# The second layer's feed-forward: one straight program for four token blocks instead of a loop with a barrier per block

## Chip, cores and metric

The kernel runs on one NeuronCore of a Trainium2 chip. The metric is the device time of one execution in microseconds (us), and less is better. TensorE is the matrix engine (PE in the profile, with PEld for its weight loads), VectorE is DVE, ScalarE is ACT, GpSimd is POOL and SyncE is SP.

## What is computed

The reference is a stack of four layers with sixteen sublayers on 2048 tokens of 128 features. After every sublayer its result is added to the running sum `x`. The change touches one sublayer, which occurs twice (after each of the second layer's two attentions):

```python
h = silu(x @ w1.T * w1_s) * (x @ w2.T * w2_s)      # 128 -> 512, "gates" and "ups"
h = gelu(h @ h1.T * h1_s)                          # 512 -> 512
h = gelu(h @ h2.T * h2_s)                          # 512 -> 512
x = x + (h @ w3.T) * w3_s                          # 512 -> 128
```

The `x` on the right of the first line is the layer-normalised running sum. The weights hold -1, 0 and 1, and everything is in float32.

## The kernel before

The running sum `X` and its normalised copy `XN` stay on chip, transposed: 128 features on the partitions and 2048 tokens along the free axis. A block is 512 tokens, so there are four blocks (`NBLK`). PSUM is one tensor `PS` with 8 banks of 128x512 float32. A float32 matmul of 128x128 weights with 128x512 tokens shows in the trace as two MATMUL records, with a weight load ahead of each.

**Stages.** The whole kernel is a sequence of stages. A stage (`stage`, line 70) gives each engine a program of its own and ends in a barrier of all engines that also clears the stage's semaphores (line 77, or line 79 for a stage without semaphores). Within a stage the engines are ordered by semaphores alone. Each engine works its own program off in order, and TensorE does not pass a matmul that waits.

**The sublayer.** `l1_ffn` (line 1133) first calls `layernorm` (line 110), a stage of its own whose last instruction is the product on VectorE at line 166. Then a hardware loop (`Fori`, line 1142) runs four times, and its body is one stage, so a barrier stands between two blocks. One block holds 44 float32 matmuls:

- TensorE: gates into banks 0 to 3 and ups into banks 4 to 7, alternating (lines 1148 and 1149, 8 matmuls); the first hidden product into banks 0 to 3 (line 1154, 16); the second hidden product into banks 4 to 7 (line 1159, 16); the last product into bank 0 (line 1163, 4).
- ScalarE: silu of the gates (line 1170), gelu after the first hidden product (line 1173) and after the second (line 1177). Silu and gelu use different function tables, so each block has two table loads.
- VectorE: the gated product of silu and ups into `HA` (line 1183), and at the end the addition to `X` (line 1186).

`l1_ffn` is called twice from `program`. After the first call comes the second attention of the layer, after the second call the next layer's feed-forward weights are loaded and the third layer begins. The SP queue and GpSimd have nothing to do in `l1_ffn` but the barriers. The weights were loaded long before.

Of the kernel before, what the change touches and what calls it, by code (L numbers as in the profile page):

```python
# [15 lines left out]
F32 = mybir.dt.float32  # L16
BF16 = mybir.dt.bfloat16
U32 = mybir.dt.uint32
ALU = mybir.AluOpType
ACT = mybir.ActivationFunctionType  # L20
AX = mybir.AxisListType

P = 128
# [3 lines left out]
NTOK = BATCH * SEQ  # L27
BLK = 512
NBLK = NTOK // BLK
# [39 lines left out]
@contextmanager  # L69
def stage(nc, *names):  # L70


    with ExitStack() as st:
        sems = [st.enter_context(nc.semaphore(n, num=STAGE_SEMS + i)) for i, n in enumerate(names)]
        yield (Programs(nc), *sems)
        if sems:
            nc.all_engine_barrier(sems_to_clear=range(STAGE_SEMS, STAGE_SEMS + len(sems)))  # L77
        else:
            nc.all_engine_barrier()


def blk(i, n=BLK):
    return slice(i * n, (i + 1) * n)
# [1047 lines left out]


def l1_ffn(k):

    nc, PS, W = k.nc, k.PS, k.W
    C = 4
    layernorm(k, k.X, k.XN)
    with ExitStack() as st:
        G = k.sbuf(st, "l1f_G", [P, C, BLK], F32)
        HA = k.sbuf(st, "l1f_HA", [P, C, BLK], F32)  # L1140
        HB = k.sbuf(st, "l1f_HB", [P, C, BLK], F32)
        with nc.Fori(0, NTOK - BLK + 1, BLK) as tb:
            with stage(nc, "g_ready", "g_done", "a_done", "h1_ready", "h1_done", "h2_ready", "h2_done", "y_ready", "added") as (block, g_ready, g_done, a_done, h1_ready, h1_done, h2_ready, h2_done, y_ready, added):
                @block.tensor
                def _(pe):
                    xn = k.XN[:, bass.ds(tb, BLK)]
                    for c in range(C):
                        nc.tensor.matmul(PS[:, c, :], W["L1_ffn_w1"][:, blk(c, P)], xn, start=True, stop=True)
                        nc.tensor.matmul(PS[:, 4 + c, :], W["L1_ffn_w2"][:, blk(c, P)], xn, start=True, stop=True).then_inc(g_ready, 1)
                    for c in range(C):  # L1150
                        pe.wait_ge(g_done, c + 1)
                        for q in range(C):
                            pe.wait_ge(a_done, q + 1)
                            mm = nc.tensor.matmul(PS[:, c, :], W["L1_ffn_h1"][:, q, blk(c, P)], HA[:, q, :], start=(q == 0), stop=(q == C - 1))  # L1154
                        mm.then_inc(h1_ready, 1)
                    for c in range(C):
                        for q in range(C):
                            pe.wait_ge(h1_done, q + 1)
                            mm = nc.tensor.matmul(PS[:, 4 + c, :], W["L1_ffn_h2"][:, q, blk(c, P)], HB[:, q, :], start=(q == 0), stop=(q == C - 1))  # L1159
                        mm.then_inc(h2_ready, 1)  # L1160
                    for q in range(C):
                        pe.wait_ge(h2_done, q + 1)
                        mm = nc.tensor.matmul(PS[:, 0, :], W["L1_ffn_w3"][:, q, :], G[:, q, :], start=(q == 0), stop=(q == C - 1))  # L1163
                    mm.then_inc(y_ready, 1)

                @block.scalar
                def _(act):
                    for c in range(C):
                        act.wait_ge(g_ready, c + 1)
                        nc.scalar.activation(G[:, c, :], PS[:, c, :], ACT.Silu, scale=W["L1_ffn_w1_s"][:, c:c + 1]).then_inc(g_done, 1)  # L1170
                    for c in range(C):
                        act.wait_ge(h1_ready, c + 1)
                        nc.scalar.activation(HB[:, c, :], PS[:, c, :], ACT.Gelu, scale=W["L1_ffn_h1_s"][:, c:c + 1]).then_inc(h1_done, 1)
                    for c in range(C):
                        act.wait_ge(h2_ready, c + 1)
                        act.wait_ge(a_done, c + 1)
                        nc.scalar.activation(G[:, c, :], PS[:, 4 + c, :], ACT.Gelu, scale=W["L1_ffn_h2_s"][:, c:c + 1]).then_inc(h2_done, 1)

                @block.vector
                def _(dve):  # L1180
                    for c in range(C):
                        dve.wait_ge(g_done, c + 1)
                        nc.vector.scalar_tensor_tensor(out=HA[:, c, :], in0=PS[:, 4 + c, :], scalar=W["L1_ffn_w2_s"][:, c:c + 1], in1=G[:, c, :], op0=ALU.mult, op1=ALU.mult).then_inc(a_done, 1)
                    dve.wait_ge(y_ready, 1)
                    xb = k.X[:, bass.ds(tb, BLK)]
                    nc.vector.scalar_tensor_tensor(out=xb, in0=PS[:, 0, :], scalar=W["L1_ffn_w3_s"], in1=xb, op0=ALU.mult, op1=ALU.add).then_inc(added, 1)  # L1186
                    dve.wait_ge(added, 1)


def l2_ffn(k):  # L1190
# [5 lines left out]
    with ExitStack() as st:  # L1196
        G = k.sbuf(st, "l2f_G", [P, C + 1, BLK], F32)
        H = k.sbuf(st, "l2f_H", [P, C + 1, BLK], F32)
        with nc.Fori(0, NTOK - BLK + 1, BLK) as tb:
            with stage(nc, "up_ready", "g_done", "h_half", "h_done", "y_ready", "added") as (block, up_ready, g_done, h_half, h_done, y_ready, added):  # L1200
# [20 lines left out]
                def _(act):  # L1221
                    for c in range(C + 1):
                        act.wait_ge(up_ready, c + 1)
                        nc.scalar.activation(G[:, c, :], PS[:, 3 * (c % 2), :], ACT.Silu).then_inc(g_done, 1)

# [646 lines left out]
def l3a(k):  # L1872

    nc, PS, W = k.nc, k.PS, k.W
    with ExitStack() as st:
        def sb(n, shape, dt=F32):
            return k.sbuf(st, n, shape, dt)
# [3 lines left out]
        S = sb("l3a_s", [P, P])  # L1881
        TRI, HB, CMASK, RMASK = sb("l3a_tri", [P, P]), sb("l3a_hb", [P, P]), sb("l3a_cmask", [P, 4, P]), sb("l3a_rmask", [P, 4])

        def layer_constants(pool, own):
            own(pool.memset(TRI[:, :], 1.0))
            own(pool.affine_select(out=TRI[:, :], in_=TRI[:, :], compare_op=ALU.is_ge, fill=0.0, base=0, pattern=[[1, P]], channel_multiplier=-1))

            own(pool.memset(HB[:, :], 1.0))
            hb = HB[:, :].rearrange("p (h d) -> p h d", d=8)
            own(pool.affine_select(out=hb, in_=hb, compare_op=ALU.is_ge, fill=0.0, base=0, pattern=[[-8, 16], [0, 8]], channel_multiplier=1))  # L1890
# [3 lines left out]
            for s in range(4):  # L1894
                own(pool.memset(CMASK[:, s, :].rearrange("p (g d) -> p g d", g=4)[:, :, 8 * s:8 * s + 8], 1.0))
            hs = HB[:, :].rearrange("p (g s d) -> p g s d", g=4, s=4)
            own(pool.tensor_tensor(RMASK[:, :], hs[:, 0, :, 0], hs[:, 1, :, 0], ALU.add))
# [2420 lines left out]
def program(nc, ins, out, first=0, last=16):  # L4318
# [3 lines left out]
    k.filled_count, k.fetched_count = 0, [0] * 8  # L4322
    run = {"l0a": l0a, "l0b": l0b, "l1a": l1a, "l1b": l1b, "l2a": l2a, "l2b": l2b, "l3a": l3a, "l3b": l3b,
           "l0_ffn": l0_ffn, "l1_ffn": l1_ffn, "l2_ffn": l2_ffn, "l3_ffn": l3_ffn}
    with ExitStack() as st:
        k.X = k.sbuf(st, "X", [P, NTOK])
# [159 lines left out]
```

## Time and profile before

| | |
|---|---|
| runs | 3692.92 us median of 3 (3684.45 to 3695.07) |
| the profiled execution's own time | 3704.39 us |
| its span in the trace | 3702.6 us |
| mean granted TensorE clock | 0.861 of full |
| TensorE busy | 2894.2 us (78%) |
| VectorE busy | 1883.8 us (51%) |
| ScalarE busy | 1402.6 us (38%) |
| GpSimd busy | 774.7 us (21%) |

The profile is one execution. Its page gives shares of the whole span; for a change in one sublayer the timeline, the table of stretches and the list of waits around that sublayer say more. In the trace the two calls of the loop stand at about 1614 to 1779 us and 2330 to 2492 us. The matmuls overlap, since they are pipelined: the end of a MATMUL record is modelled, and the distance between two starts is the rate.

### The profile page before, as it was taken

To read this page: it belongs to the slowest core of one execution; us is meant where nothing else is said; L and a number is where in the kernel's file an instruction comes from. 1 tells how busy PE (TensorE), PEld (TensorE's weight loads), DVE (VectorE), ACT (ScalarE), POOL (GpSimd) and SP (SyncE) were. 2 spreads that over 40 slices of the span, in tenths; PEclk is the share of its full clock that TensorE was granted. 3 is DMA by queue.
4 is the path that set the end of the run, shared out by engine and by line. 5 is a ranking of instruction groups with operands and counts; after the bars stand their busy time and mean duration, and the time that the engine had idled before them with its cause. 6 is when DMAs were issued, how large, how long until landed. Compare 5 with 4: busy or idle time off the path is not lost. (4 is left out here: it accounts for less than half of the span.)

```text
span 3702.6 us, 55144 instructions
## 1 busy us (share of the span) xinstructions
PE 2894.2 (78%) x21390; PEld 1513.0 (41%) x21458; DVE 1883.8 (51%) x3574; ACT 1402.6 (38%) x2678; POOL 774.7 (21%) x631
## 2 busy tenths in 40 slices
PE   6566777778877599989768888998878568777986
PEld 3454247423367334434322222332333333554545
DVE  4311253388953388710488877103953543626733
ACT  3211423433233256632366776323122112234652
POOL 1000006146526200000544320003610000240003
PEclk9666879878878789989889999997999779887987
DMA  2022001122111412000132200000600001014202
GB/s 105 15 68 65 0 16 42 34 75 68 40 27 42 114 36 41 15 0 0 28 53 31 30 2 1 0 11 26 161 7 0 0 0 46 13 54 79 46 11 68
DMA packets 86471, 136.29 MB, mean 37 GB/s; under 512 B 13319, under 2 KB 52199, under 8 KB 84947
## 3 DMA queue, kind: packets, MB, share of 16 engines
q1 hardware_dynamic: 79187, 118.50, 13.0%
q0 software_dynamic: 7040, 14.43, 1.5%
q8 instruction: 165, 2.70, 0.3%
q14 instruction: 79, 0.65, 0.1%
HBM read 106.81 MB, written 25.85 MB: 36 GB/s over the span
## 5 line engine op out<-in xcount | busy, mean ns | idle before, releaser
L1608 ACT ACTIVATE at_pt<-PS 128x384 f32<-128x384 f32 (+3 forms) x704 | 288.7, 455 | 237.4 <-PE PS L1520 202.1
L1658 DVE TENSOR_REDUCE at_mp<-PS 128x1 f32<-128x384 f32 (+3 forms) x640 | 313.5, 538 | 114.9 <-PE PS L1508 98.8
L1505 PE MATMUL PS<-at_kx,at_qx 72*128 72x384 bf16 (+5 forms) x640 | 219.0, 347 | 66.7 <-DMA at_kx<-L_attn_a_parts 26.7
L1518 PE MATMUL PS<-at_qx,at_kx 105*128 105x512 bf16 (+5 forms) x704 | 214.4, 314 | 7.8 <-ACT at_pt L1608 5.9
L4146 DVE CUSTOM_DVE_ANT_0 PS<-PS,ls_pt 128x1024 f32<-128x1024 f32 x128 | 153.9, 1239 | 18.4 <-ACT ls_pt L3999 15.6
L3999 ACT ACTIVATE ls_pt<-PS,ls_far 128x512 f32<-128x512 f32 x256 | 155.0, 686 | 20.4 <-PE PS L3820 11.7
L2271 DVE TENSOR_TENSOR_SCAN mb_ring<-PS,mb_ring 128x1024 f32<-128x1024 f32 x64 | 146.6, 2291 | 18.9 <-POOL mb_ring L2210 6.7
L2226 PE MATMUL PS<-mb_ring,ident 128*128 128x512 f32 x256 | 147.2, 727 | 6.1 <-DVE mb_ring L2276 6.0
L989 ACT ACTIVATE mx_h<-PS,small_L 128x128 f32<-128x128 f32 x312 | 88.2, 372 | 151.5 <-PE PS L873 60.7
L873 PE MATMUL PS<-mx_g,mx_w 128*128 128x128 f32 x624 | 100.7, 313 | 50.9 <-DVE mx_w L1066 24.9
L2255 ACT ACTIVATE PS<-mb_dt,mb_a 128x1024 f32<-128x1024 f32 x64 | 71.6, 1118 | 174.8 <-DVE mb_ring L2271 169.5
L1531 PE MATMUL PS<-at_pt,at_v 128*9 128x256 f32 (+3 forms) x1408 | 130.7, 451 | 5.5 <-issue 1.4
L1520 PE MATMUL PS<-at_above,identb 128*128 128x128 bf16 x704 | 133.8, 223 | 0.0
L1508 PE MATMUL PS<-at_above,identb 128*128 128x128 bf16 x704 | 131.5, 233 | 0.0
L1505 PEld LDWEIGHTS PS<-at_kx,at_qx 102*128 102x128 bf16 (+1 forms) x640 | 64.7, 101 | 159.7 <-DVE at_mp L1658 85.2
L1186 DVE SCALAR_TENSOR_TENSOR X<-PS,small_L,X 128x512 f32 x8 | 6.0, 751 | 236.2 <-PE PS L1163 236.2
L873 PEld LDWEIGHTS PS<-mx_g,mx_w 128*128 128x128 f32 x624 | 90.9, 224 | 58.3 <-DVE mx_w L1066 49.8
L1154 PE MATMUL PS<-l1f_HA,ffn_place 128*128 128x512 f32 x256 | 111.2, 592 | 0.0
L1159 PE MATMUL PS<-l1f_HB,ffn_place 128*128 128x512 f32 x256 | 111.2, 592 | 0.0
L166 DVE TENSOR_TENSOR XN<-PS,lnA 128x512 f32<-128x512 f32 x56 | 38.7, 692 | 138.6 <-ACT lnA L148 138.6
L2217 PE MATMUL PS<-mb_xd,mb_selc 40*128 40x512 f32 x128 | 71.3, 681 | 41.2 <-DVE mb_ring L2276 31.1
L3827 PE MATMUL PS<-ls_kx,ls_qx 96*128 96x512 bf16 x256 | 79.1, 391 | 29.0 <-DVE ls_mp L4146 24.0
(803 smaller groups left out, 6545.8 us busy)
## 6 DMA issues: line engine op xcount, KB each, us to landing
rw_arena<-rw_v_rows SPq DMA_DIRECT2D x32, 512.0 KB, 4.7
dl_arena<-in_fir_bank SPq DMA_DIRECT2D x32, 256.0 KB, 3.1
lnA<-mb_rows SPq DMA_DIRECT2D x16, 512.0 KB, 3.7
XN<-mb_rows SPq DMA_DIRECT2D x16, 512.0 KB, 3.6
ffn_place<-in_ffn_L SPq DMA_DIRECT2D x4, 1152.0 KB, 17.3
at_qx<-L_attn_a_parts SPq DMA_DIRECT2D x24, 192.0 KB
at_kx<-L_attn_a_parts SPq DMA_DIRECT2D x72, 64.0 KB
at_qx<-L_attn_b_parts SPq DMA_DIRECT2D x24, 192.0 KB
```

What stands on the lines that cost most here:

```text
L873: mm = nc.tensor.matmul(PS[:, n % 4, blk(c, P)], W1[:, n % 3, blk(c, P)], XG[:, n % 2, :], start=True, stop=True)
L1505: mm = nc.tensor.matmul(PS[:, n % 3, 0:e - c], QX[0:RAW, u % 3, g, blk(i, P)], KX[0:RAW, u % 3, g, c:e], start=True, stop=True)
L1508: mm = nc.tensor.matmul(PS[:, n % 3, j * P - c:(j + 1) * P - c], k.identb[:, :], ABOVE[:, 0 if j >= i else 1, :], start=False, stop=True, ...
L1518: mm = nc.tensor.matmul(PS[:, 3 + n % 3, 0:e - c], KX[0:FULL, u % 3, g, blk(j, P)], QX[0:FULL, u % 3, g, c:e], start=True, stop=True)
L1520: mm = nc.tensor.matmul(PS[:, 3 + n % 3, i * P - c:(i + 1) * P - c], k.identb[:, :], ABOVE[:, 1 if i <= j else 0, :], start=False, stop=Tr ...
L1531: mm = nc.tensor.matmul(PS[32 * g:32 * g + 9, 6, c - BLK * h:e - BLK * h], V1[:, NT * (u // 4) + j, HG * (u % 4) + g, :], PT[:, (G2 * u + ...
L1608: nc.scalar.activation(PT[:, y % SLOTS, g, 0:e - c], PS[:, 3 + n % 3, 0:e - c], ACT.Exp, scale=SCALE).then_inc(exp_done, 1)
L1658: nc.vector.tensor_reduce(best, sc, AX.X, ALU.max).then_inc(s_maxed, 1)
L2226: mm = nc.tensor.matmul(PS[:, 2 * h + t, :], k.ident[:, :], HC[:, m % 3, blk(t)], start=(n == 0), stop=(n == NS - 1))
L2271: nc.vector.tensor_tensor_scan(HS, wide(6), BU[:, m % 3, :], 0.0, ALU.mult, ALU.add).then_inc(scanned, 1)
L3999: nc.scalar.activation(PT[x % 4][:, blk(t)], PS[:, 4 + (2 * x + t) % 3, :], ACT.Relu, bias=far[:, 0:1], scale=NEG).then_inc(pen_done, 1)
L4146: nc.vector.tensor_tensor_reduce(wide(bank), wide(bank), PT[x % 4], 1.0, -3e38, ALU.subtract, ALU.max, MP[:, u % 2, i // HALF, g, i % HALF ...
```

## The change

The loop and the barrier after each block go. Each engine gets one program over all four blocks, inside one stage, with semaphore values that count on from block to block. There is one more buffer, `S`, for the silu, which shared `G` before. On TensorE the next block's gates stand ahead of the last product of the block before (`gates`, `third`, `ups`, `first`, `second`), and the ups follow that product. The ups now go to banks 5, 6, 7 and 4, and the last product goes to bank 4 in place of bank 0. The additions to `X` stand on VectorE ahead of the next block's gated products. The diff, with removed lines that are in the listing above left out:

```diff
@@ -1131,60 +1131,107 @@
 def l1_ffn(k):
...
     nc, PS, W = k.nc, k.PS, k.W
     C = 4
     layernorm(k, k.X, k.XN)
     with ExitStack() as st:
-        G = k.sbuf(st, "l1f_G", [P, C, BLK], F32)
-        HA = k.sbuf(st, "l1f_HA", [P, C, BLK], F32)
-        HB = k.sbuf(st, "l1f_HB", [P, C, BLK], F32)
-        with nc.Fori(0, NTOK - BLK + 1, BLK) as tb:
-            with stage(nc, "g_ready", "g_done", "a_done", "h1_ready", "h1_done", "h2_ready", "h2_done", "y_ready", "added") as (block, g_ready, g_done, a_done, h1_ready, h1_done, h2_ready, h2_done, y_ready, added):
...
-                    xn = k.XN[:, bass.ds(tb, BLK)]
+        S, HA, HB, G = (k.sbuf(st, "l1f_" + n, [P, C, BLK], F32) for n in ("S", "HA", "HB", "G"))
+        UP_BANK = (5, 6, 7, 4)
+        with stage(nc, "s_ready", "s_done", "up_ready", "a_done", "h1_ready", "h1_done", "h2_ready", "h2_done", "y_ready", "added") as (block, s_ready, s_done, up_ready, a_done, h1_ready, h1_done, h2_ready, h2_done, y_ready, added):
+            @block.tensor
+            def _(pe):
+                def gates(b):
                     for c in range(C):
...
+                        if b:
+                            pe.wait_ge(h1_done, C * (b - 1) + c + 1)
+                        nc.tensor.matmul(PS[:, c, :], W["L1_ffn_w1"][:, blk(c, P)], k.XN[:, blk(b)], start=True, stop=True).then_inc(s_ready, 1)
+                def ups(b):
                     for c in range(C):
...
+                        if b:
+                            pe.wait_ge(h2_done, C * (b - 1) + C)
+                        if b and c == C - 1:
+                            pe.wait_ge(added, b)
+                        nc.tensor.matmul(PS[:, UP_BANK[c], :], W["L1_ffn_w2"][:, blk(c, P)], k.XN[:, blk(b)], start=True, stop=True).then_inc(up_ready, 1)
+                def first(b):
+                    for c in range(C):
+                        pe.wait_ge(s_done, C * b + c + 1)
                         for q in range(C):
...
+                            pe.wait_ge(a_done, C * b + q + 1)
                             mm = nc.tensor.matmul(PS[:, c, :], W["L1_ffn_h1"][:, q, blk(c, P)], HA[:, q, :], start=(q == 0), stop=(q == C - 1))
                         mm.then_inc(h1_ready, 1)
+                def second(b):
                     for c in range(C):
                         for q in range(C):
...
+                            pe.wait_ge(h1_done, C * b + q + 1)
                             mm = nc.tensor.matmul(PS[:, 4 + c, :], W["L1_ffn_h2"][:, q, blk(c, P)], HB[:, q, :], start=(q == 0), stop=(q == C - 1))
                         mm.then_inc(h2_ready, 1)
+                def third(b):
                     for q in range(C):
...
+                        pe.wait_ge(h2_done, C * b + q + 1)
+                        mm = nc.tensor.matmul(PS[:, 4, :], W["L1_ffn_w3"][:, q, :], G[:, q, :], start=(q == 0), stop=(q == C - 1))
                     mm.then_inc(y_ready, 1)
...
+                for b in range(NBLK):
+                    gates(b)
+                    if b:
+                        third(b - 1)
+                    ups(b)
+                    first(b)
+                    second(b)
+                third(NBLK - 1)
+            @block.scalar
+            def _(act):
+                def silu(b):
                     for c in range(C):
...
+                        act.wait_ge(s_ready, C * b + c + 1)
+                        if b:
+                            act.wait_ge(a_done, C * (b - 1) + c + 1)
+                        nc.scalar.activation(S[:, c, :], PS[:, c, :], ACT.Silu, scale=W["L1_ffn_w1_s"][:, c:c + 1]).then_inc(s_done, 1)
+                def first(b):
                     for c in range(C):
...
+                        act.wait_ge(h1_ready, C * b + c + 1)
+                        if b and c == 0:
+                            act.wait_ge(h2_ready, C * b)
                         nc.scalar.activation(HB[:, c, :], PS[:, c, :], ACT.Gelu, scale=W["L1_ffn_h1_s"][:, c:c + 1]).then_inc(h1_done, 1)
+                def second(b):
                     for c in range(C):
...
+                        act.wait_ge(h2_ready, C * b + c + 1)
+                        if b and c == 0:
+                            act.wait_ge(y_ready, b)
                         nc.scalar.activation(G[:, c, :], PS[:, 4 + c, :], ACT.Gelu, scale=W["L1_ffn_h2_s"][:, c:c + 1]).then_inc(h2_done, 1)
...
+                for b in range(NBLK):
+                    silu(b)
+                    first(b)
+                    second(b)
+            @block.vector
+            def _(dve):
+                def product(b):
                     for c in range(C):
...
-                    xb = k.X[:, bass.ds(tb, BLK)]
...
+                        dve.wait_ge(s_done, C * b + c + 1)
+                        dve.wait_ge(up_ready, C * b + c + 1)
+                        if b and c == 0:
+                            dve.wait_ge(h1_ready, C * b)
+                        nc.vector.scalar_tensor_tensor(out=HA[:, c, :], in0=PS[:, UP_BANK[c], :], scalar=W["L1_ffn_w2_s"][:, c:c + 1], in1=S[:, c, :], op0=ALU.mult, op1=ALU.mult).then_inc(a_done, 1)
+                def add(b):
+                    dve.wait_ge(y_ready, b + 1)
+                    nc.vector.scalar_tensor_tensor(out=k.X[:, blk(b)], in0=PS[:, 4, :], scalar=W["L1_ffn_w3_s"], in1=k.X[:, blk(b)], op0=ALU.mult, op1=ALU.add).then_inc(added, 1)
+                for b in range(NBLK):
+                    if b:
+                        add(b - 1)
+                    product(b)
+                add(NBLK - 1)
+                dve.wait_ge(added, NBLK)
 def l2_ffn(k):
```

## Rows read from the trace of the kernel before

**Rows 1.** The page: the head, and busy us by engine.

```profile
span 3702.6 us, 55144 instructions
...
PE 2894.2 (78%) x21390; PEld 1513.0 (41%) x21458; DVE 1883.8 (51%) x3574; ACT 1402.6 (38%) x2678; POOL 774.7 (21%) x631
```

**Rows 2.** Stretches, one per block; columns: busy us by engine, granted clock, DMA share, GB/s.

```profile
1655.50:1697.30 41.80, 39.73 (x88) 17.21 (x88) 3.75 (x5) 10.82 (x14) 0.00 (x0) 0.96 0.00 0
1697.30:1737.30 40.00, 38.03 (x88) 16.64 (x88) 3.75 (x5) 10.81 (x14) 0.00 (x0) 1.00 0.00 0
...
2450.30:2492.00 41.70, 39.73 (x88) 17.23 (x88) 3.76 (x5) 10.81 (x14) 0.00 (x0) 0.96 0.00 0
```

**Rows 3.** Timeline, first seam of call 1; columns: start, duration, engine, instruction, [idle before].

```profile
1650.96 3.60 PE L1163 MATMUL PS<-l1f_G,ffn_place 128*128 128x512 f32 x8
...
1651.17 0.69 ACT L1177 ACTIVATE l1f_G<-PS,small_L 128x512 f32<-128x512 f32 x1 [2.75 <-PE PS L1159]
...
1654.70 0.75 DVE L1186 SCALAR_TENSOR_TENSOR X<-PS,small_L,X 128x512 f32 x1 [29.53 <-PE PS L1163]
...
1656.61 1.83 PE L1148 MATMUL PS<-XN,ffn_place 128*128 x2 [2.04 <-PEq L77]
...
1665.27 13.90 PE L1154 MATMUL PS<-l1f_HA,ffn_place 128*128 128x512 f32 x32
```

**Rows 4.** Timeline, call 1, block 3: its first matmuls and its first hidden product.

```profile
1698.34 1.12 PE L1148 MATMUL PS<-XN,ffn_place 128*128 x2 [2.01 <-PEq L77]
...
1705.31 13.90 PE L1154 MATMUL PS<-l1f_HA,ffn_place 128*128 128x512 f32 x32
```

**Rows 5.** Line 1148, whole kernel: what ended TensorE's idle time before it.

```profile
  PEq L77: 17.8, 8
```

**Rows 6.** Timeline, block 1 of both calls: layernorm's end, first matmuls, hidden products, table load, last gated product.

```profile
1612.36 0.69 DVE L166 TENSOR_TENSOR XN<-PS,lnA 128x512 f32<-128x512 f32 x1 [0.64 <-ACT lnA L148]
...
1613.80 2.07 PE L1148 MATMUL PS<-XN,ffn_place 128*128 x2 [2.86 <-PEq L77]
...
1623.50 13.90 PE L1154 MATMUL PS<-l1f_HA,ffn_place 128*128 128x512 f32 x32
...
1624.40 1.28 ACT L1173 ACT_TABLE_LOAD   x1
1624.42 0.75 DVE L1183 SCALAR_TENSOR_TENSOR l1f_HA<-PS,small_L,l1f_G 128x512 f32<-128x512 f32 x1 [0.97 <-ACT l1f_G L1170]
...
1637.23 13.90 PE L1159 MATMUL PS<-l1f_HB,ffn_place 128*128 128x512 f32 x32
...
2329.80 2.07 PE L1148 MATMUL PS<-XN,ffn_place 128*128 x2 [2.85 <-PEq L77]
...
2338.20 13.90 PE L1154 MATMUL PS<-l1f_HA,ffn_place 128*128 128x512 f32 x32
```

**Rows 7.** Timeline, the last addition of call 1 and of call 2.

```profile
1778.22 0.75 DVE L1186 SCALAR_TENSOR_TENSOR X<-PS,small_L,X 128x512 f32 x1 [29.52 <-PE PS L1163]
...
2491.22 0.75 DVE L1186 SCALAR_TENSOR_TENSOR X<-PS,small_L,X 128x512 f32 x1 [29.52 <-PE PS L1163]
```

**Rows 8.** Short stretches over the first seam of call 1 (columns as in rows 2).

```profile
1654.40:1656.60 2.20, 0.16 (x1) 0.00 (x0) 0.75 (x1) 0.42 (x1) 0.00 (x0) 1.00 0.00 0
1656.60:1658.60 2.00, 1.99 (x3) 0.96 (x4) 0.00 (x0) 0.86 (x1) 0.00 (x0) 0.57 0.00 0
1658.60:1660.60 2.00, 2.00 (x4) 0.72 (x3) 0.00 (x0) 0.41 (x1) 0.00 (x0) 0.58 0.00 0
```

**Rows 9.** Long dense stretches of other sublayers, and one full of instructions (columns as in rows 2).

```profile
2000.00:2300.00 300.00, 261.73 (x1343) 84.37 (x1366) 246.25 (x332) 222.51 (x389) 85.46 (x32) 1.00 0.13 19
3390.00:3510.00 120.00, 113.86 (x1238) 70.72 (x1245) 81.10 (x204) 74.39 (x191) 0.00 (x0) 1.00 0.27 45
...
100.00:200.00 100.00, 62.62 (x3086) 53.79 (x3087) 26.88 (x43) 19.05 (x31) 0.00 (x0) 0.72 0.05 15
```

**Rows 10.** DMA queues, 100 to 200 us: kind, packets, MB, share of 16 engines.

```profile
q8 instruction: 24, 0.39, 1.6%
```

More of the change, by code:

```diff
@@ L1138, in l1_ffn @@
     with ExitStack() as st:
-        G = k.sbuf(st, "l1f_G", [P, C, BLK], F32)
-        HA = k.sbuf(st, "l1f_HA", [P, C, BLK], F32)
-        HB = k.sbuf(st, "l1f_HB", [P, C, BLK], F32)
-        with nc.Fori(0, NTOK - BLK + 1, BLK) as tb:
-            with stage(nc, "g_ready", "g_done", "a_done", "h1_ready", "h1_done", "h2_ready", "h2_done", "y_ready", "added") as (block, g_ready, g_done, a_done, h1_ready, h1_done, h2_ready, h2_done, y_ready, added):
-                @block.tensor
-                def _(pe):
-                    xn = k.XN[:, bass.ds(tb, BLK)]
+        S, HA, HB, G = (k.sbuf(st, "l1f_" + n, [P, C, BLK], F32) for n in ("S", "HA", "HB", "G"))
@@ L1147, in _ @@
+        UP_BANK = (5, 6, 7, 4)
[3 more added lines that the diff above has]
+                def gates(b):
                     for c in range(C):
-                        nc.tensor.matmul(PS[:, c, :], W["L1_ffn_w1"][:, blk(c, P)], xn, start=True, stop=True)
@@ L1149, in _ @@
-                        nc.tensor.matmul(PS[:, 4 + c, :], W["L1_ffn_w2"][:, blk(c, P)], xn, start=True, stop=True).then_inc(g_ready, 1)
+                        if b:
+                            pe.wait_ge(h1_done, C * (b - 1) + c + 1)
+                        nc.tensor.matmul(PS[:, c, :], W["L1_ffn_w1"][:, blk(c, P)], k.XN[:, blk(b)], start=True, stop=True).then_inc(s_ready, 1)
+                def ups(b):
                     for c in range(C):
-                        pe.wait_ge(g_done, c + 1)
+                        if b:
[3 more added lines that the diff above has]
+                        nc.tensor.matmul(PS[:, UP_BANK[c], :], W["L1_ffn_w2"][:, blk(c, P)], k.XN[:, blk(b)], start=True, stop=True).then_inc(up_ready, 1)
@@ L1152, in _ @@
+                def first(b):
+                    for c in range(C):
+                        pe.wait_ge(s_done, C * b + c + 1)
                         for q in range(C):
-                            pe.wait_ge(a_done, q + 1)
+                            pe.wait_ge(a_done, C * b + q + 1)
                             mm = nc.tensor.matmul(PS[:, c, :], W["L1_ffn_h1"][:, q, blk(c, P)], HA[:, q, :], start=(q == 0), stop=(q == C - 1))
                         mm.then_inc(h1_ready, 1)
+                def second(b):
@@ L1156, in _ @@
                     for c in range(C):
                         for q in range(C):
-                            pe.wait_ge(h1_done, q + 1)
+                            pe.wait_ge(h1_done, C * b + q + 1)
                             mm = nc.tensor.matmul(PS[:, 4 + c, :], W["L1_ffn_h2"][:, q, blk(c, P)], HB[:, q, :], start=(q == 0), stop=(q == C - 1))
                         mm.then_inc(h2_ready, 1)
+                def third(b):
                     for q in range(C):
-                        pe.wait_ge(h2_done, q + 1)
@@ L1163, in _ @@
-                        mm = nc.tensor.matmul(PS[:, 0, :], W["L1_ffn_w3"][:, q, :], G[:, q, :], start=(q == 0), stop=(q == C - 1))
+                        pe.wait_ge(h2_done, C * b + q + 1)
+                        mm = nc.tensor.matmul(PS[:, 4, :], W["L1_ffn_w3"][:, q, :], G[:, q, :], start=(q == 0), stop=(q == C - 1))
                     mm.then_inc(y_ready, 1)
-                @block.scalar
-                def _(act):
-                    for c in range(C):
-                        act.wait_ge(g_ready, c + 1)
-                        nc.scalar.activation(G[:, c, :], PS[:, c, :], ACT.Silu, scale=W["L1_ffn_w1_s"][:, c:c + 1]).then_inc(g_done, 1)
+                for b in range(NBLK):
[5 more added lines that the diff above has]
+                    second(b)
@@ L1171, in _ @@
+                third(NBLK - 1)
+            @block.scalar
+            def _(act):
+                def silu(b):
+                    for c in range(C):
+                        act.wait_ge(s_ready, C * b + c + 1)
[3 more added lines that the diff above has]
+                def first(b):
                     for c in range(C):
-                        act.wait_ge(h1_ready, c + 1)
+                        act.wait_ge(h1_ready, C * b + c + 1)
+                        if b and c == 0:
+                            act.wait_ge(h2_ready, C * b)
@@ L1173, in _ @@
                         nc.scalar.activation(HB[:, c, :], PS[:, c, :], ACT.Gelu, scale=W["L1_ffn_h1_s"][:, c:c + 1]).then_inc(h1_done, 1)
+                def second(b):
                     for c in range(C):
-                        act.wait_ge(h2_ready, c + 1)
-                        act.wait_ge(a_done, c + 1)
+                        act.wait_ge(h2_ready, C * b + c + 1)
+                        if b and c == 0:
+                            act.wait_ge(y_ready, b)
                         nc.scalar.activation(G[:, c, :], PS[:, 4 + c, :], ACT.Gelu, scale=W["L1_ffn_h2_s"][:, c:c + 1]).then_inc(h2_done, 1)
-                @block.vector
@@ L1180, in _ @@
-                def _(dve):
-                    for c in range(C):
-                        dve.wait_ge(g_done, c + 1)
-                        nc.vector.scalar_tensor_tensor(out=HA[:, c, :], in0=PS[:, 4 + c, :], scalar=W["L1_ffn_w2_s"][:, c:c + 1], in1=G[:, c, :], op0=ALU.mult, op1=ALU.mult).then_inc(a_done, 1)
-                    dve.wait_ge(y_ready, 1)
-                    xb = k.X[:, bass.ds(tb, BLK)]
-                    nc.vector.scalar_tensor_tensor(out=xb, in0=PS[:, 0, :], scalar=W["L1_ffn_w3_s"], in1=xb, op0=ALU.mult, op1=ALU.add).then_inc(added, 1)
-                    dve.wait_ge(added, 1)
+                for b in range(NBLK):
+                    silu(b)
+                    first(b)
+                    second(b)
```

## The prediction

> **What bounds the kernel now.** I read the page's head first [rows 1]: TensorE is the busiest engine with 78% of the span, but that is a mean over sixteen sublayers, so it does not say what a seam between two blocks of one sublayer is worth. Next the stretches, one per block [rows 2]. In all eight blocks TensorE is busy 38.0 to 40.8 of 40.0 to 41.8 us, VectorE 3.8 us and ScalarE under 11 us, and no DMA runs. So TensorE alone sets the time of this sublayer, and what it does not do at full rate is what can be won. The granted clock differs between blocks: 1.00 in the block of the second row, 0.96 in the two others. Then the timeline at the seam [rows 3]: the last product's eight records start at 1650.96 and end 3.60 us later, at 1654.56; the addition to X follows from 1654.70 to 1655.45; then comes the barrier, and at 1656.61 the next block's first matmul, after 2.04 us of idle time. Inside a block there is no idle time at all: 32 records of the first hidden product start at 1623.50 and the next group at 1637.23 [rows 6], 13.73 us for 32, or 0.4291 us from start to start. A record lasts 0.59 us, so each overlaps the next by 0.16 us.
>
> **Sum, by what a call would take without seams.** A block is 44 matmuls, 88 records. Four blocks in one stream are 352 x 0.4291 = 151.04 us. To this I add what the change leaves in place. The first 16 records of a call run partly at the low clock: 1613.80 to 1623.50 is 9.70 us in call 1 and 2329.80 to 2338.20 is 8.40 us in call 2 [rows 6], against 16 x 0.4291 = 6.87, so 2.83 and 1.53 us too long. At the end stand the last record's overlap of 0.16, the 0.14 to the addition and its 0.75: 1.05 us. New call 1: 151.04 + 2.83 + 1.05 = 154.92. New call 2: 151.04 + 1.53 + 1.05 = 153.62. Old calls, from the first matmul to the end of the last addition: 1613.80 to 1778.97 is 165.17 us, and 2329.80 to 2491.97 is 162.17 us [rows 6, 7]. Saved: 10.25 + 8.55 = **18.8 us**.
>
> **The same sum by parts.** (a) Idle time at the seams. TensorE sat idle 17.8 us ahead of the eight blocks' first matmuls [rows 5]; 2.86 and 2.85 of it are ahead of block 1 of each call [rows 6] and stay, 12.1 us are the six seams. In a continuous stream each would also overlap by 0.16, 6 x 0.16 = 1.0. Together 13.1 us. (b) The low clock behind a seam. In the first seam the clock was still full while TensorE sat idle and stood at 0.57 and 0.58, that is mostly at 1.2 GHz, for the next 4 us [rows 8]. The first 16 records took 1656.61 to 1665.27 = 8.66 us there [rows 3], 1.79 more than 6.87, but 1698.34 to 1705.31 = 6.97 us behind the next seam [rows 4], 0.10 more. Three of the six seams are of the first kind (the blocks at 0.96 behind a seam: two are shown, the third is block 4 of call 1) and three of the second: 5.7 us. 13.1 + 5.7 = 18.8, as above.
>
> The Trainium skill (TensorE: Matmul & The Clock Gate, section on HAM oscillation) blames longer pauses than these for a fall to the low clock; by that rule the 5.7 us would not be tied to the seams, and the sum would be 13.1. Rows 8 speak against it, since the fall follows a pause of 2.04 us, so I keep both parts; that it would not be tied to them is rival 1.
>
> **What the change adds, and where it hides.** I count from T, the moment at which a next record could follow the last one of the second hidden product. *Gates ahead of the last product:* moved, not added; 4 x 0.858 = 3.43 us of matmuls. They wait for gelus that were read 13.7 us earlier, and write banks 0 to 3, which nobody reads any more. They also cover the last gelu of the block, which starts 0.21 us after T and ends at T + 0.90 [rows 3]. *Silu:* the last gelu, a table load of 1.28 and four silus of 0.69 end at T + 4.9; the first gated product can't start before the first up has ended, at T + 3.43 + 3.43 + 0.86 + 0.16 = T + 7.9. Three us of cover; without it, the gap on TensorE would be what is late. The gelu table load follows the silus as it does now [rows 6]. *Addition ahead of the gated products:* the last product ends at T + 6.86 + 0.16, the addition takes 0.14 + 0.75 and ends at T + 7.9, just as the first up is ready. Nothing is queued behind it that is due sooner. *The new wait of the fourth up for the addition (bank 4):* it is due at T + 6.86 + 2.57 = T + 9.4, 1.5 us after the addition. Were it late, the ups' last matmul and all first hidden products would queue behind it. *Gated products:* the fourth up ends at T + 10.45, its product at T + 11.4, and the first hidden product wants it at T + 10.29 + 2.57 = T + 12.9. Now the last gated product of a block ends at 1625.17 and is wanted at 1623.50 + 2.57 = 1626.07 [rows 6], so the slack grows from 0.9 to 1.5. *Waits:* more of them per matmul, none with a row of its own. Two waits already stand ahead of line 1154's matmuls and the pitch there is 0.4291, so I take zero; the other end is a fresh start's 0.10 [rows 4] at each of the 16 groups of gates and ups, 1.6 us. A gain is excluded, since nothing shortens the pitch. *Buffer S, the `Fori` and its register work:* nothing but the seam itself. *Start of the first block:* from the layernorm's end (1613.05) to the first matmul (1613.80) is 0.75 us [rows 6]; nothing in it is the loop's for certain, I take zero, at most 0.75 a call. The step back from block to block is 1655.45 to 1656.61 = 1.16 us [rows 3]; all of it is in part (a).
>
> **The longer program.** The loop's body was held once and is now there four times. Elsewhere 6173 TensorE instructions in 100 us came with 24 instruction packets of 0.39 MB [rows 9, 10], 64 bytes or so each. A call is 4 x 176 = 704 instructions in about 151 us, a thirteenth of that rate. I take zero; one packet late by a seam's worth of 2 us, for two or three packets a call, makes the other end, 10 us.
>
> **Behind the sublayer** the rest moves up as a whole, since a barrier ends every stage and no transfer is under way. Its share of low clock can fall out differently; the three runs spread over 10.6 us, so I allow 5 us either way.
>
> **The number.** The profiled execution's own time is 3704.39 us, so it would be 3685.6. That is 11.5 above the median of the runs shown (3692.92), to which the same 18.8 us apply: **3674.1 us**. A measurement of this kernel can tell about 0.3%, 11 us, from no change; the boundary lies at 3681.8.
>
> **Rivals.** *1. The clock part does not come back.* The low clock falls into the longer stream or the stage behind it. For: it shows behind only three seams of six that look alike. Against: rows 8, and the blocks' inner stretches without any. Saves 13.1: 3679.8 us. *2. The seam goes but something takes its place*, code fetch or the chain addition, fourth up, gated product. It would have to cost over 1.3 us at each of six block borders to bring the saving below 11: say half of the 18.8, 3683.5 us. Against: the slacks of 1.5 us and the thirteenth of a rate that runs elsewhere. *3. Slower: the stream is too dense.* TensorE now runs 151 us twice without a pause, and the granted clock could sag under it. Price: 302 / g - 302. It eats the 18.8 at a mean clock g of 0.94 and goes past 11 us slower at 0.91; at 0.90 it is 33.6, so 3707.7 us. Against: 120 us with TensorE busy 95% and 300 us with 87% both stood at 1.00 [rows 9]. The Trainium skill (same page, Part 1, the peak-current limiter) says that one or two busy cores never trip the chip's limit for dense matmuls; by that this rival is out, and rows 9 agree as far as they go. *4. The change doesn't do what it says*, a pause stays at each border: like 2.
>
> **Chances.** Forecast 0.62, rival 1 0.20, rivals 2 and 4 together 0.13, rival 3 0.03, something outside both ways 0.02. The forecast with its 5 us is 3669 to 3679 and lies wholly under 3681.8; rival 1 lies under it two times in three; of the rest most is within 0.3%. That gives faster 0.80, same 0.16, slower 0.04. The range takes in the forecast, rival 1 and the better half of rival 2, with the median's own spread: 3663 to 3686.
>
> **What would show it.** In the changed trace: TensorE without idle time at the three inner borders of each call, and a first-to-last time near 155 and 154 us; granted clock 1.00 in every stretch after the first 6 us of a call; the last product's records directly behind four gate matmuls; the fourth up 0.4291 behind its neighbour; additions ending near T + 7.9 and silus near T + 4.9. A pause ahead of the fourth up or of the first hidden product means rival 2; low clock inside a call, rival 1 or 3. The forecast is wrong if a call still takes over 158 us, or if both calls are short and the whole is not.

## The result, and the profile after

The changed kernel takes 3670.61 us (median of 7 runs, 3661.11 to 3674.99) beside 3692.92 us for the kernel before (7 runs), a ratio of 0.9944 with a 95% interval of 0.9929 to 0.9958. By the ratio that is 20.7 us less, between 15.5 and 26.2; the two medians differ by 22.3. Forecast were 3674.1 us and 18.8 us less. The profiled execution took 3664.16 us. A second comparison of the same two kernels (e10) gave 0.9963 (0.9947 to 0.9979), and the two intervals overlap from 0.9947 to 0.9958, 15 to 20 us.

The head of the page after, busy us by engine, and its instruction queues:

```profile
span 3662.2 us, 54986 instructions
...
PE 2882.8 (79%) x21390; PEld 1511.2 (41%) x21458; DVE 1884.3 (51%) x3574; ACT 1399.7 (38%) x2678; POOL 769.0 (21%) x631
...
q8 instruction: 169, 2.77, 0.3%
q14 instruction: 82, 0.66, 0.1%
```

The same 21390 matmul records as in [rows 1]; what went is time between them and, where the clock was low, time in them (busy is 11.4 us less). The stretches of call 1, one per block's worth of 88 records (columns: width, busy us and count of PE, PEld, DVE, ACT and POOL, granted clock, DMA share, GB/s), which answer to [rows 2]:

```profile
1607.60:1645.40 37.80, 37.76 (x88) 16.83 (x89) 3.00 (x4) 13.24 (x17) 0.00 (x0) 1.00 0.00 0
1645.40:1683.20 37.80, 37.80 (x89) 16.72 (x88) 3.75 (x5) 10.51 (x16) 0.00 (x0) 1.00 0.00 0
1683.20:1721.00 37.80, 37.80 (x89) 16.72 (x88) 3.75 (x5) 10.52 (x16) 0.00 (x0) 1.00 0.00 0
1721.00:1759.80 38.80, 37.95 (x89) 16.53 (x87) 4.51 (x6) 7.98 (x12) 0.00 (x0) 1.00 0.00 0
```

TensorE is busy for 37.8 us of each of the first three, and the clock stands at 1.00 throughout; 40.0 to 41.8 us became 37.8. The timeline of the first inner border, which answers to [rows 3] (line 1169 is the second hidden product, 1147 the gates, 1175 the last product, 1155 the ups, 1194 the silu, 1223 the gated product, 1227 the addition):

```profile
1642.05 3.60 PE L1147 MATMUL PS<-XN,ffn_place 128*128 128x512 f32 x8
...
1642.25 0.69 ACT L1208 ACTIVATE l1f_G<-PS,small_L 128x512 f32<-128x512 f32 x1 [2.75 <-PE PS L1169]
...
1642.96 1.28 ACT L1194 ACT_TABLE_LOAD   x1
...
1644.25 2.42 ACT L1194 ACTIVATE l1f_S<-PS,small_L 128x512 f32<-128x512 f32 x4
...
1645.48 3.60 PE L1175 MATMUL PS<-l1f_G,ffn_place 128*128 128x512 f32 x8
...
1648.92 3.60 PE L1155 MATMUL PS<-XN,ffn_place 128*128 128x512 f32 x8
...
1649.12 0.75 DVE L1227 SCALAR_TENSOR_TENSOR X<-PS,small_L,X 128x512 f32<-128x512 f32 x1 [33.51 <-PE PS L1175]
...
1650.03 3.34 DVE L1223 SCALAR_TENSOR_TENSOR l1f_HA<-PS,small_L,l1f_S 128x512 f32<-128x512 f32 x4 [0.16 <-PE PS L1155]
```

No PE row has a bracket, so none had idle time before it. With T = 1642.05, the silus end at T + 4.6, the addition at T + 7.8 and the last gated product at T + 11.3. The ends of both calls (timelines, first matmuls and last additions):

```profile
1607.64 3.67 PE L1147 MATMUL PS<-XN,ffn_place 128*128 128x512 f32 x8 [2.53 <-PEq L77]
...
1758.99 0.75 DVE L1227 SCALAR_TENSOR_TENSOR X<-PS,small_L,X 128x512 f32<-128x512 f32 x1 [30.08 <-PE PS L1175]
...
2307.70 3.67 PE L1147 MATMUL PS<-XN,ffn_place 128*128 128x512 f32 x8 [2.53 <-PEq L77]
...
2459.04 0.75 DVE L1227 SCALAR_TENSOR_TENSOR X<-PS,small_L,X 128x512 f32<-128x512 f32 x1 [30.08 <-PE PS L1175]
```

**Where the time went.** The profiled spans differ by 40.4 us, more than the medians. In call 1, 165.17 became 152.10 (13.1), in call 2, 162.17 became 152.09 (10.1). The rest is ahead of call 1 (6.2), between the calls (2.9) and behind them (8.2), where but for the loop's entry and exit the programs are the same. That such a rest is spread between executions, and not the change, is seen in the other traces: in the profiles of the kernel before, the changed one (twice), e1, e2 and e8, which share that code, the stretch behind call 2 took 1202.4 to 1218.2 us, and the one between the calls 544.9 to 550.8.

### The profile page after: what moved, and what is told of

Read it like the earlier page. It is cut to its first block and busy times, and to the rows that moved or that the text cites. A ratio compares the mean times of both kernels' runs of the same rounds, so it can differ in the third digit from the quotient of the medians.

```text
span 3662.2 us, 54986 instructions
## 1 busy us (share of the span) xinstructions
PE 2882.8 (79%) x21390; PEld 1511.2 (41%) x21458; DVE 1884.3 (51%) x3574; ACT 1399.7 (38%) x2678; POOL 769.0 (21%) x631
## 5 line engine op out<-in xcount | busy, mean ns | idle before, releaser
L2318 DVE TENSOR_TENSOR_SCAN mb_ring<-PS,mb_ring 128x1024 f32<-128x1024 f32 x64 | 146.6, 2291 | 18.8 <-POOL mb_ring L2257 6.6
```

The costliest lines, as they stand in the source:

```text
L2318: nc.vector.tensor_tensor_scan(HS, wide(6), BU[:, m % 3, :], 0.0, ALU.mult, ALU.add).then_inc(scanned, 1)
```

## The experiments

"A call" is the time from its first matmul to the end of its last addition to X, read off the timeline as above. "Low" counts the inner borders, of the six in two calls, behind which the granted clock fell. The pause, the calls and "low" are read from one profiled execution of each kernel. Each ratio is to the kernel before on the same chip. Of e6, e7 and e8 there is one run each (3702.76, 3687.39 and 3698.28 us); eleven runs of the kernel before on that chip lie between 3684.31 and 3707.02, so these three times say nothing of the change, and only their traces are used.

| | pause at a border | call 1, call 2 | low | ratio (95%) |
|---|---|---|---|---|
| before | 2.0 | 165.17, 162.17 | 3 of 6 | |
| changed | 0 | 152.10, 152.09 | 0 | 0.9944 (0.9929 to 0.9958) |
| e1, barriers without loop | 1.31 | 156.73, 156.73 | 0 | 0.9983 (0.9965 to 1.0) |
| e2, last product first | 0 | 152.10, 153.79 | 0 | 0.9954 (0.9937 to 0.997) |
| e4, pause | 1.63 | 160.68, 159.26 | 0 | 0.9997 (0.9983 to 1.0012) |
| e5, long pause | 3.99 | 175.30, 171.53 | 6 of 6 | 1.0077 (1.0045 to 1.0108) |
| e6, pause | 2.15 | 161.04, 161.04 | 2 of 6 | one run |
| e7, pause | 2.42 | 164.81, 161.71 | 2 of 6 | one run |
| e8, bank 4 for the first up | 0.94 | 158.58, 155.62 | 0 | one run |
| e9, also the third layer's loop | 0 | 155.01, 152.10 | 0 | 0.9919 (0.9897 to 0.9941) |
| e10, changed, again | 0 | 155.10, 153.79 | 0 | 0.9963 (0.9947 to 0.9979) |
| e11, e9 again | 0 | 152.10, 153.68 | 0 | 0.9921 (0.9894 to 0.9948) |

**e1: the barrier without the loop.**

```diff
-        with nc.Fori(0, NTOK - BLK + 1, BLK) as tb:
+        for tb in range(0, NTOK, BLK):
...
-                    xn = k.XN[:, bass.ds(tb, BLK)]
+                    xn = k.XN[:, tb:tb + BLK]
```

> The kernel before with its hardware loop written out: four stages with a barrier each, same order within a block. My theory: most of a seam is the barrier itself, and the loop's step back adds some 0.4 us to each (0.75 us from the layernorm's end to the first matmul, 1.16 us from block to block), its entry and exit another 0.3 each. TensorE idle 1.3 to 1.7 us at each of the six seams in place of 2.0, a call 156.5 to 158 us at full clock plus up to 1.8 us behind each seam where the clock falls; the whole 3 to 6 us under before, about 3688. Rival (the loop is what costs: branch and code for it): the seams nearly close and the time comes near the changed kernel, 3673.

Timeline of its first seam:

```profile
1619.56 0.75 DVE L1186 SCALAR_TENSOR_TENSOR X<-PS,small_L,X 128x512 f32<-128x512 f32 x1 [29.43 <-PE PS L1163]
...
1620.83 1.10 PE L1148 MATMUL PS<-XN,ffn_place 128*128 128x512 f32 x2 [1.31 <-PEq L77]
```

The pause is 1.31 us against 2.04 in [rows 3] and 2.01 on the mean of the six seams before. So 0.70 us of a seam was the loop's step, not the 0.4 I had read off, and 1.31 the addition and the barrier. The step takes in the reading of the block's address from the loop's register, which the edit removes with the loop; the two are not told apart. No border had low clock behind it. By the traces a call costs 4.6 us more than the changed kernel's, 3 x 1.55. So writing the loop out alone, with the barriers kept, brings the clock part and a third of the pauses. The measured ratio, 6 us less than before and between 0 and 13, agrees with the 10 or 11 us of the traces (with block 1's clock left out) and doesn't fix them.

**e2: the last product ahead of the gates.**

```diff
                 for b in range(NBLK):
-                    gates(b)
                     if b:
                         third(b - 1)
+                    gates(b)
                     ups(b)
```

> The changed kernel with one swap: the last product of a block stands ahead of the next block's gates again. My theory: the gates ahead of it hide nothing that needs hiding (the last gelu ends 0.9 us after the second hidden product, the last product wants it after 2.6 us), so a call stays at 152.1 us at full clock and the whole at 3671 within the noise of some 5 us. Rival (the reorder carries part of the gain): a pause shows ahead of the last product or of the ups, 0.5 us or more at each of six borders, 3 us or more in all.

```profile
1613.67 3.60 PE L1175 MATMUL PS<-l1f_G,ffn_place 128*128 128x512 f32 x8
...
1617.10 3.60 PE L1147 MATMUL PS<-XN,ffn_place 128*128 128x512 f32 x8
...
1617.31 0.75 DVE L1227 SCALAR_TENSOR_TENSOR X<-PS,small_L,X 128x512 f32<-128x512 f32 x1 [30.08 <-PE PS L1175]
...
1620.54 3.60 PE L1155 MATMUL PS<-XN,ffn_place 128*128 128x512 f32 x8
```

Again no idle time on TensorE (timeline, first inner border), and call 1 takes 152.10, to the hundredth what the changed kernel's takes; call 2's 1.7 more stand in block 1, at low clock. The moved gates bring nothing here: the one program, with this choice of banks, brings it all.

**e4 to e7: pauses without loop or barrier.** On e2's order, TensorE waits at each border until the addition and one (e4), two (e6: one of them half as wide; e7) or four (e5) more VectorE instructions are done. Their results go to a buffer that is free by then, and nothing of the computation is left out. In e5:

```diff
                         third(b - 1)
+                        pe.wait_ge(added, 5 * b)
                     gates(b)
...
+                    for m in range(1, 5):
+                        dve.wait_ge(added, 5 * b + m)
+                        nc.vector.scalar_tensor_tensor(out=k.lnA[:, blk(b)], in0=PS[:, 4, :], scalar=W["L1_ffn_w3_s"], in1=k.XN[:, blk(b)], op0=ALU.mult, op1=ALU.add).then_inc(added, 1)
```

> One program as in e2_last_first, but TensorE waits at each block border until the addition and one more VectorE instruction of the same form behind it are done: a pause of about 1.9 us with no barrier and no loop. My theory: a seam costs its pause and what low clock follows it, whatever makes the pause: a call 158 to 164 us, low clock (mean about 0.96 over a block) behind some of the six borders and not behind others; the whole 12.4 us over e2 plus 0 to 11, so 3683 to 3694, and nearest 3689. Rival 1 (the low clock has nothing to do with pauses of 2 us): all blocks at 1.00, calls at 158.3, 3683.

> The same with four more VectorE instructions, a pause of about 4.5 us at each border. My theory: low clock behind nearly every border, for 2 to 5 us each; a call 166 us from pauses alone (152.1 + 3 x 4.7) and 170 to 172 with the clock; the whole near 3671 + 28 + 6 x 1.8 = 3710. Rival 1: calls at 166, the whole at 3699, and 1.00 in all blocks.

> One program with neither loop nor barrier, and at each border a pause of about 2.0 to 2.1 us (the addition, one VectorE instruction of its size, one of half its size), as long as the seam of the kernel before. So far: pauses of 1.31 us (e1) and 1.63 us (e4) had no low clock behind any of twelve borders, those of 2.0 us (before) behind three of six, those of 4.0 us (e5) behind six of six. My theory (the length of the pause decides, not what makes it): low clock behind 2 to 4 of the six borders, calls 158.5 to 162. Rival (the loop's step or the barrier itself brings it): 1.00 at all borders, calls at 158.6 and no more than block 1 can add, which is up to 3 us.

> The same with a pause of about 2.4 us (three full VectorE instructions). My theory: low clock behind more of the borders than in e6, 3 to 6 of six; calls 152.1 + 3 x 2.6 = 159.9 and 1.7 to 1.8 us more for each such border. Rival: 1.00 at all borders, 159.9.

The stretches of 6.8 us, each from the start of the last record ahead of a pause, some 0.6 us before TensorE falls idle; e4's first and last border, e5's first two, then all six of e6:

```profile
1621.60:1628.40 6.80, 5.17 (x13) 2.17 (x12) 1.50 (x2) 2.86 (x5) 0.00 (x0) 1.00 0.00 0
...
2405.50:2412.30 6.80, 5.17 (x13) 2.15 (x12) 1.50 (x2) 2.85 (x5) 0.00 (x0) 1.00 0.00 0
```

```profile
1621.70:1628.50 6.80, 2.81 (x5) 1.18 (x4) 3.75 (x5) 0.18 (x1) 0.00 (x0) 0.72 0.00 0
1666.40:1673.20 6.80, 2.81 (x5) 1.17 (x4) 3.75 (x5) 0.23 (x1) 0.00 (x0) 0.70 0.00 0
```

```profile
1649.80:1656.60 6.80, 4.65 (x12) 1.88 (x11) 1.99 (x3) 2.35 (x4) 0.00 (x0) 1.00 0.00 0
1690.00:1696.80 6.80, 4.65 (x8) 1.74 (x7) 1.99 (x3) 1.34 (x2) 0.00 (x0) 0.75 0.00 0
1731.90:1738.70 6.80, 4.65 (x12) 1.91 (x11) 1.99 (x3) 2.39 (x4) 0.00 (x0) 1.00 0.00 0
2364.00:2370.80 6.80, 4.65 (x12) 1.92 (x11) 1.99 (x3) 2.39 (x4) 0.00 (x0) 1.00 0.00 0
2404.20:2411.00 6.80, 4.65 (x12) 1.94 (x11) 1.99 (x3) 2.41 (x4) 0.00 (x0) 1.00 0.00 0
2444.40:2451.20 6.80, 4.65 (x8) 1.80 (x7) 1.99 (x3) 1.37 (x2) 0.00 (x0) 0.75 0.00 0
```

TensorE is busy for the same 4.65 us in all six of e6, but in two stretches with 8 records in place of 12. Since e6 has neither loop nor barrier, its pauses alone bring the low clock. Over all kernels: pauses of 0.94, 1.31 and 1.63 us had it behind 0 of 18 borders, 2.0 to 2.4 us behind 7 of 18, 4.0 us behind 6 of 6. At 2.42 it was no more frequent than at 2.0, against what I expected of e7 (3 to 6, found 2), so in between the length alone doesn't settle it; what else does is left open here. e4 by itself came out as its rival 1 had it, 1.00 at all borders, and only the longer pauses turned the verdict. Its calls add up: 152.10 + 3 x (1.63 + 0.16 + 0.10 for a fresh start) = 157.8, plus 2.9 and 1.5 in block 1, and its median is 13.5 us over e2's on the same chip (3660.32 and 3646.83), near the 11.3 of its six pauses (6 x 1.89; the 12.4 expected stood for pauses of 1.9 us). Against the kernel before, its two calls are 7.4 us shorter in the traces, but the ratio says 1 us less, between 6 less and 4 more. The kernel before may thus have had fewer low borders on the mean of its runs than the three of its one profile; no run shows that. e5's median (3691.13) is 44 us over e2's, above the 39 that I had summed and well above rival 1's 28; its two calls, with block 1's low clock left out, are 39.7 us over the changed kernel's.

**e8: the first up waits for the addition.**

```diff
-        UP_BANK = (5, 6, 7, 4)
+        UP_BANK = (4, 5, 6, 7)
...
-                        if b and c == C - 1:
+                        if b and c == 0:
```

> The changed kernel with the ups in banks 4, 5, 6, 7 in place of 5, 6, 7, 4, so that the first up, not the fourth, waits for the addition, which ends about 1.0 us after it is due. My theory of the slack: a pause ahead of the ups of 0.8 to 0.9 us idle (one VectorE instruction and what lies around it) at each of six borders, no low clock behind it; a call 152.1 + 3 x 1.0 = 155.1. Rival (an order of instructions can hide it on another engine): 152.1.

```profile
1663.94 0.75 DVE L1227 SCALAR_TENSOR_TENSOR X<-PS,small_L,X 128x512 f32<-128x512 f32 x1 [33.51 <-PE PS L1175]
...
1664.84 3.67 PE L1155 MATMUL PS<-XN,ffn_place 128*128 128x512 f32 x8 [0.94 <-DVE X L1227]
```

The timeline of its first border shows the wait where the sum puts it: 0.94 us idle, released by the addition. Call 2 is 155.62, 3.5 over 152.09, so 1.18 a border. By the traces the order of the banks is worth 7 us over two calls; the addition does end about 1 us after the first up is due, and so ahead of the fourth, which in the changed trace is due 1.6 us after it (1.5 in the prediction).

**e9 and e11: the same for the third layer's feed-forward; e10: the changed kernel again.** In `l2_ffn` the loop and its stage become one program in the same manner, with chunks counted on over the blocks (`n = N * b + c`), `H` doubled and the output in bank 6 or 7:

```diff
-        with nc.Fori(0, NTOK - BLK + 1, BLK) as tb:
-            with stage(nc, "up_ready", "g_done", "h_half", "h_done", "y_ready", "added") as (block, up_ready, g_done, h_half, h_done, y_ready, added):
...
+                for b in range(NBLK):
+                    ups(b, 0)
+                    if b:
+                        down(b - 1)
+                    for c in range(1, N):
+                        ups(b, c)
+                down(NBLK - 1)
```

> The changed kernel, and the third layer's feed-forward, the other sublayer with such a loop, written in the same way: one program for four blocks, the first chunk of a block ahead of the down products of the block before, twice the buffers for H and two output banks. Its seams have TensorE idle 1.9 us each, six in two calls. From the first theory: 6 x (1.92 + 0.16) = 12.5, entry and exit of the loops 1.2, and low clock behind some seams 0 to 5: 14 to 19 us under the changed kernel; against the kernel before a ratio near 0.990. Rival (the gain of the first change was partly luck of the clock and does not repeat): ratio 0.993 to 0.995.

> The changed kernel once more, as the other end for e11 on one chip. Both calls 152.1 us or up to 3 us more where block 1 starts at the low clock, which it did in 9 of 20 calls so far; no idle time and no low clock at the inner borders. Ratio to the kernel before 0.9935 to 0.995. Rival (the gain was partly luck of one profile): low clock inside a call, or a ratio over 0.996.

> e9 once more, beside the changed kernel. From the traces: the third layer's two calls take 13.2 us less apart from the clock, so 13 us under e10 within some 6, ratio to the kernel before 0.990 to 0.992. Rival (given back later): within 5 us of e10.

The timeline of e9 at the border of the third layer's first two blocks (the first three rows, of lines 1255, 1256 and 1258, are the second block's first chunk, line 1267 is the first block's down products, and the last row the second block's next chunk):

```profile
2751.75 1.12 PE L1255 MATMUL PS<-XN,ffn_place 128*128 128x512 f32 x2 [0.22 <-DVE l2f_H L1304]
2752.71 1.02 PE L1256 MATMUL PS<-XN,ffn_place 128*128 128x512 f32 x2
2753.66 1.12 PE L1258 MATMUL PS<-gates,sel 16*128 16x512 f32 x2
2754.72 4.56 PE L1267 MATMUL PS<-l2f_H,ffn_place 128*128 128x512 f32 x10
2759.11 1.02 PE L1255 MATMUL PS<-XN,ffn_place 128*128 128x512 f32 x2
```

Of the pause of 1.9 us at this border 0.22 us is left, a wait for a product on VectorE (line 1304). e11 takes 3629.53 us where e10 takes 3645.15 on the same chip, 15.6 less, against 13 expected within 6, and every run of e11 lies under every run of e10. With both sublayers written out the ratios are 0.9919 and 0.9921. e9 by itself did not decide: 0.9919 lies between the 0.990 of my theory and the 0.993 to 0.995 of its rival, and its interval reaches both; e11 beside e10 on one chip decides it. e10 itself came out at 0.9963, above the 0.9935 to 0.995 that I had written and with the rival's "over 0.996". So of the rival's two marks the one in the ratio came true, and the gain may well be under the first comparison's 20.7 us. The one in the trace did not: there is no idle time and no low clock at an inner border. The trace has the low clock in block 1 of both calls (timeline, call 1):

```profile
1581.02 6.67 PE L1147 MATMUL PS<-XN,ffn_place 128*128 128x512 f32 x8 [2.53 <-PEq L77]
...
1587.53 2.74 PE L1155 MATMUL PS<-XN,ffn_place 128*128 128x512 f32 x6
```

The eight gate records took 6.67 us here and 3.67 in the first profile.

## Why the prediction was right

- **The bound.** TensorE alone, as read: with the pauses out, a call is the 151.04 + 1.05 us of the sum, measured 152.10 and 152.09. e2, e9 and e11 repeat it.
- **Idle time at the seams, 13.1.** Shown: 12.1 us of idle time are 0 after, and each pause put back costs its length and 0.16 for the overlap, plus 0.07 to 0.10 for a fresh start (a call is 3 x 1.55 us longer in e1, 3 x 1.18 in e8). What I had not seen is its make-up: 0.70 of 2.01 us was the loop's step.
- **Low clock behind seams, 5.7; rival 1.** Shown by e6 and by what e1, e4, e8 and the changed kernel lack: the low clock came with pauses of 2 us or more, not with loop or barrier, and did not move elsewhere in the stream. In ten calls without inner pauses (changed, e2, e9, e10, e11) there is none behind block 1. It did not move behind the stream either: the mean granted clock was 0.94 between the calls before and after the change, and 0.77 in both over the first 20 us behind call 1. The size is less sure than the cause. Three borders of six were one execution's draw; at the 7 of 18 of all borders with 2.0 to 2.4 us the part would be some 4 us, an estimate, and no comparison here is fine enough to tell 4 from 5.7. The rule of the Trainium skill that I weighed (TensorE: Matmul & The Clock Gate, section on HAM oscillation), by which only longer pauses bring it, does not hold here: the measurements at 2.0 to 2.4 us decide.
- **Block 1 at low clock, 2.83 + 1.53, left in place.** This is the term that failed in the first profile, where both calls start at full clock. It is drawn anew in each execution: 12 of the 24 calls in all profiles have it, for 1.5 to 3.0 us. I took one execution's draw for a fixed cost; it is a spread of some 3 us around the whole.
- **The loop's entry and exit, taken at 0.** They were 0.33 us (layernorm's end to first matmul 0.75 before, 0.42 after) a call, and at the exit (last addition's end to the next stage's first matmul) 0.27 us behind call 1 (0.79 and 0.52) and 0.14 behind call 2 (2.86 and 2.72), 1.1 us in all: a small loss in the sum, on the safe side.
- **The longer program.** Two more q8 instruction packets in call 1's stretch (3 against 1), 4 in the whole page, and not one gap between 352 records: zero, as taken. Rivals 2 and 4 fall with it.
- **Added waits, silu, addition, bank 4.** Ends at T + 4.6, 7.8 and 11.3 against 4.9, 7.9 and 11.4. e8 shows what bank 4 costs without its cover. That the gates ahead of the last product hide nothing follows from the slack that I wrote, but I did not say so: this part of the change is worth nothing (e2).
- **Rival 3.** Granted clock 1.00 over both streams of 151 us.
- **The whole.** 18.8 us lie in the intervals of all three comparisons of this structure (the changed kernel's two and e2's). One can't see from 20.7, 13.6 and 16.8 which is nearest; the traces give 18.8 + 1.1 and the draw of block 1. The idle time at the seams is calculated and shown. That the whole came within 2 us of the first comparison is in part luck, since the sum took two draws of one execution, the low clock in block 1 and behind three seams, as fixed.

## What to carry to other kernels

A barrier between blocks of a sublayer that one engine bounds costs its pause on that engine, and the low clock that may follow: price both from the rows at the seam, and take the loop's own step apart from the barrier (here 0.70 us, and 1.31 with the addition), since writing the loop out is the smaller edit and here already takes the pause under the lengths at which the clock fell. Before reordering instructions across the border, count the slack: here both orders tried did, while one choice of bank cost 1.2 us a border. For a gain of half a per cent, judge by the stretch in the trace, and by medians only across comparisons; executions of the kernel before on one chip spread over 33 us here (3639.30 to 3672.62), more than the change brought.

## What the runs showed of the hardware

- TensorE's granted clock fell behind pauses of 2.0 to 2.4 us in 7 of 18 cases, in none of 18 up to 1.63 us, in 6 of 6 at 4.0 us. Each fall cost some 1.7 us of matmul time at the shorter pauses (e6: 161.04 - 152.10 - 3 x 2.41), and 2.2 to 2.5 on average at the long ones (e5).
- A barrier between two written-out stages left TensorE idle for 1.31 us including the 0.75 us addition ahead of it; the same barrier with a hardware loop's step 2.0 us.
- The same kernel before took 3692.92, 3661.97, 3693.19 and 3663.70 us (medians) in four comparisons, up to 31 us apart, while the ratios hold to some 0.2%.
